# A transformer block with two recurrences: x times W_ih for up to four steps at once, kept in an SBUF ring

## The reference, cut to what matters

```
def cell(h, x):                                   # GRU, one time step
    i_r, i_z, i_n = split(x @ W_ih + b_ih, 3)     # x: 64 x 512, W_ih: 512 x 1536
    h_r, h_z, h_n = split(h @ W_hh + b_hh, 3)
    r, z = sigmoid(i_r + h_r), sigmoid(i_z + h_z)
    n = tanh(i_n + r * h_n)
    return (1 - z) * n + z * h

def derivative(q, p, drive):                      # oscillators
    dq = q - q**3 / 3 - p + drive + tanh(q) @ coupling.T + bias
    dp = EPSILON * (q + ALPHA - BETA * p)
# four derivatives (Runge-Kutta) and a clip for each time step;
# drive of step t is x + (the GRU's h of step t)
```

## Time and profile before

| | |
|---|---|
| median of three runs | 1514.97 us (1504.56 to 1516.10) |
| the profiled execution | 1517.27 us, its span 1515.2 us |
| granted TensorE clock, mean | 0.988 |
| TensorE busy | 1453.9 us, 96% |
| VectorE busy | 1275.0 us, 84% |
| ACT busy | 902.3 us, 60% |
| GpSimd busy | 768.6 us, 51% |

### The profile page before, as it was taken

One profiled execution on the slowest core, in us unless ns is written; L12 is line 12 of the kernel. 1 busy time (PEld: TensorE's weight loads), 2 busy tenths in 40 slices (PEclk: granted clock), 3 DMA queues, 4 the chain that ended last, 5 costly groups with the idle time before them and its releaser, 6 DMA issues.

```text
span 1515.2 us, 94439 instructions
## 1 busy us (share of the span) xinstructions
PE 1453.9 (96%) x41966; PEld 1279.7 (84%) x41966; DVE 1275.0 (84%) x3095; ACT 902.3 (60%) x2753; POOL 768.6 (51%) x916
## 2 busy tenths in 40 slices
PE   4799999999999999999999999999999999999997
PEld 2366766666766669999999999999999999999996
DVE  6888888778888776788888889889888888888887
ACT  5567766757767743555555555555555555555553
POOL 2567777757677756443444344344444434434432
PEclk8899999999999999999999999999999999999999
DMA  7477777767777772000000000000000000000000
GB/s 258 82 158 167 162 154 161 166 146 169 170 171 176 153 163 79 12 11 15 15 12 15 15 12 15 15 12 15 16 15 11 15 15 12 15 15 12 15 15 14
DMA packets 188216, 108.74 MB, mean 72 GB/s; under 512 B 134272, under 2 KB 165184, under 8 KB 187808
## 3 DMA queue, kind: packets, MB, share of 16 engines
q1 hardware_dynamic: 187360, 102.45, 28.7%
q10 hardware_dynamic: 448, 0.25, 0.1%
HBM read 50.65 MB, written 11.67 MB: 41 GB/s over the span
## 4 chain that ended last, share of the span: by engine, by line
PE 79%; DVE 9%; DMA 4%; issue 3%; SPq 2%; ACT 1%; POOL 1%; DVEq 0%; ACTq 0%; POOLq 0%
PE psB L1463 35%; PE psA L1492 15%; PE psQ L1174 10%; PE psA L1497 8%; PE psQ L1220 4%; PE psO L1266 3%; DMA first<-qn 2%; DMA PT<-front 2%; PE psO L1254 2%; PE psB L1202 1%; DVE psA L830 1%; SPq L325 1%; DVE qn L770 1%; DVE room L801 1%; DVE oT L893 1%
## 5 line engine op out<-in xcount | busy, mean ns | idle before, releaser
L1463 PE MATMUL psB<-first,Wx 128*128 128x64 f16 x9216 | 290.7, 193 | 1.8 <-issue 1.3
L1492 PE MATMUL psA<-ts,Cp 128*128 128x64 f16 x8160 | 281.0, 193 | 7.1 <-ACT ts L1563 6.4
L1463 PE MATMUL psB<-first,Whh 128*128 128x64 f16 x9072 | 286.2, 193 | 0.8 <-POOL first L1928 0.5
L1174 PE MATMUL psQ<-Wx,front 128*128 128x512 f16 x1152 | 280.1, 391 | 5.5 <-DVE front L982 4.6
L1463 PEld LDWEIGHTS psB<-first,Wx 128*128 128x128 f16 x9216 | 278.0, 98 | 2.8 <-issue 2.4
L1463 PEld LDWEIGHTS psB<-first,Whh 128*128 128x128 f16 x9072 | 273.7, 98 | 1.4 <-POOL first L1928 0.6
L1492 PEld LDWEIGHTS psA<-ts,Cp 128*128 128x128 f16 x8160 | 256.3, 98 | 8.3 <-ACT ts L1563 7.2
L1563 ACT ACTIVATE ts<-qst 128x256 f16<-128x256 f32 x192 | 80.1, 417 | 298.0 <-DVE qst L1676 298.0
L1174 PEld LDWEIGHTS psQ<-Wx,front 128*128 128x128 f16 x1152 | 107.5, 100 | 124.3 <-issue 12.3
L1928 POOL TENSOR_TENSOR en<-rz,dn 128x256 f32<-128x256 f32 x64 | 46.7, 730 | 259.5 <-issue 256.8
L1497 PE MATMUL psA<-ts,Cp 128*128 128x64 f16 x4080 | 161.2, 193 | 0.0
(11 more groups left out here) (199 smaller groups left out, 2899.8 us busy)
## 6 DMA issues: line engine op xcount, KB each, us to landing
rows<-rows_dram SPq DMA_DIRECT2D x64, 256.0 KB, 4.3
front<-in_x SPq DMA_DIRECT2D x32, 256.0 KB, 4.3
XR<-in_x_turned SPq DMA_DIRECT2D x32, 256.0 KB, 4.8
out<-ob SPq DMA_DIRECT2D x63, 128.0 KB, 1.8
x<-x SPq DMA_DIRECT2D x29, 224.0 KB
Whh<-in_W_qkv SPq DMA_DIRECT2D x12, 256.0 KB, 8.3
room<-in_W_hh SPq DMA_DIRECT2D x12, 256.0 KB, 2.7
room<-in_W_ih SPq DMA_DIRECT2D x12, 256.0 KB, 2.9
```

The lines of the kernel that those rows point to most:

```text
L1174: last = mm(psQ[:, n, :], xn[p.u][:, i, c, :], Wqkv[:, j, c, n * D:(n + 1) * D], start=(c == 0 and t == 0), stop=(c == KC - 1 and t == 2))
L1463: last = mm(o, W_[:, i, c, g * PART:(g + 1) * PART], src[:, j, c, :], start=False, stop=False, skip_group_check=True)
L1492: mm(psF[:, s % 2, m, :], Cp[:, i, c, m * PART:(m + 1) * PART], ts_[:, 0, c, :], start=(c == 0 and m == 0 and i == 0), stop=False, skip_gr ...
```

## The change

x times W_ih leaves the gates' PSUM. The cells 3 to 62 are put in groups (`CELLS`): [3], [4, 5], [6, 7], twelve groups of four from 8 to 55, [56, 57], [58, 59], [60], [61], [62]. The products of a group are made together, with up to 4 x 64 = 256 columns, into one of two banks of psQ (`products_of_group`), in the steps of `STEPS_OF`: group 0 in step 0, group 1 in step 1, group 2 in steps 2 and 3, group 3 (cells 8 to 11) in steps 4 and 5, the groups of cells 12 to 55 in four steps each (6 to 49), [56, 57] in steps 50 to 53, [58, 59] in 54 and 55, [60] in 56 and 57, [61] in 58, [62] in 59, none in 60. A group has 12 chunks of 12 products; a step does 12 divided by the number of its group's steps, the first half of them between stages 0 and 1, the rest between stages 1 and 2. ACT copies each chunk with its bias to the SBUF ring gx (`keep`), the first half of a step's chunks behind tanh_n and the others behind seed_n. A chunk waits until the chunk two before it has been copied. Cells 0 to 2 and 63 stay as they were. `seed_rz` copies from gx, `seed_n` seeds h's half alone, gate_b adds from gx. seed_n now stands behind high_h and the square of stage 2. The square sq and PA move to SBUF, nn to the half of psN that x's part held. In the front three pairs of semaphores are merged into two, with the same waits.

```diff
+    LEN = 4
+    CELLS = [[3], [4, 5], [6, 7]] + [list(range(n, n + LEN)) for n in range(8, 56, LEN)] + [[56, 57], [58, 59], [60], [61], [62]]
+    xg = [sb(f"xg{u}", [PART, 2, KC, LEN, B], F16) for u in range(2)]
+    gx = [sb(f"gx{u}", [PART, GC, LEN, B]) for u in range(2)]
+    GROUP = {n: g for g, cells in enumerate(CELLS) for n in cells}
+    STEPS_OF = [[0]] + [list(range(CELLS[g - 1][0] - 2, CELLS[g][0] - 2)) for g in range(1, len(CELLS))]
+    assert sorted(GROUP) == list(range(3, T - 1)) and sum(STEPS_OF, []) == list(range(T - 4))
+
+    def chunks_in(n):
+        for g, steps in enumerate(STEPS_OF):
+            if n in steps:
+                per = GC // len(steps)
+                return g, range(steps.index(n) * per, (steps.index(n) + 1) * per)
+        return None, range(0)
+
+    def turned_in(n):
+        for g, steps in enumerate(STEPS_OF):
+            if n in steps:
+                cells = CELLS[g + 1] if g + 1 < len(CELLS) else [T - 1]
+                return [c for k, c in enumerate(cells) if steps[k * len(steps) // len(cells)] == n]
+        return []
+
+    def place_of(n):
+        g = GROUP[n] if n < T - 1 else len(CELLS)
+        return g, (n - CELLS[g][0] if n < T - 1 else 0)
+
+    def xs_of(n):
+        if n < 3:
+            return xs1 if n == 1 else xs
+        g, k = place_of(n)
+        return xg[g % 2][:, :, :, k, :]
...
-    psRZ, psN, psF, psT, psQ, psH, psE = (bank(*k) for k in (("psB", 0), ("psB", 1), ("psA", 0), ("psA", 1), ("psQ", 0), ("psQ", 1), ("psQ", 2)))
+    psRZ, psN, psF, psT, psE = (bank(*k) for k in (("psB", 0), ("psB", 1), ("psA", 0), ("psA", 1), ("psQ", 2)))
+    psX = banks["psQ"]
     psS = banks["psO"][:, :, :].rearrange("p c n -> p (c n)").rearrange("p (v c b) -> p v c b", v=2, c=KC)
-    th, sq = psT[:, 0, :, :], psQ[:, 0, :, :]
-    nn, PA = psH[:, 0, :, :], psH[:, 1, :, :]
+    th, sq = psT[:, 0, :, :], sb("sqs", F)[:, :, :]
+    nn, PA = psN[:, 1, :, :], sb("PA", F)[:, :, :]
...
+        def products_of_group(g, parts):
+            N = len(CELLS[g]) * B if parts else 0
+            for m, c in parts:
+                j = g * GC + m
+                if c == 0:
+                    if m == 0:
+                        pe.wait_ge(S["xs_ready"], CELLS[g][-1] + 1)
+                    need(pe, S["gx_kept"], j - 1)
+                for k, (i, jj) in enumerate(TERMS):
+                    last = mm(psX[:, j % 2, 0:N], Wih[:, i, c, m * PART:(m + 1) * PART],
+                              xg[g % 2][:, jj, c, :, :].rearrange("p t b -> p (t b)")[:, 0:N],
+                              start=(c == 0 and k == 0), stop=(c == KC - 1 and k == 2), skip_group_check=True)
+                if c == KC - 1:
+                    last.then_inc(S["gx_done"], 1)
...
         def step(t):
+            g, ms = chunks_in(t.n)
+            parts = [(m, c) for m in ms for c in range(KC)]
             if t.n:
                 stage(t, 0)
-            gi_front(t.n + 2)
+            if t.n == 0:
+                gi_front(2)
+            products_of_group(g, parts[:len(parts) // 2])
             stage(t, 1)
-            gi_back(t.n + 2)
+            if t.n == 0:
+                gi_back(2)
+            products_of_group(g, parts[len(parts) // 2:])
             stage(t, 2)
+            pe.wait_ge(S["seeded_rz"], t.n + 3)
+            pe.wait_ge(S["seeded_n"], t.n + 3)
             gh_front(t.n + 2)
...
-                act.wait_ge(S["gi_done"], n)
-            a((xs1 if n == 1 else xs)[:, 0, :, :].rearrange("p c b -> p (c b)"), xr(n)).then_inc(S["xs_hi"], 1)
+                need(act, S["gx_done"], (place_of(n)[0] - 1) * GC)
+            a(xs_of(n)[:, 0, :, :], XR[:, :, :, n]).then_inc(S["xs_hi"], 1)
 
         def seed_rz(n):
             need(act, S["sig_done"], n)
-            a(both(psRZ), both(seedRZ)).then_inc(S["seeded_rz"], 1)
+            if n in GROUP:
+                g, k = place_of(n)
+                act.wait_ge(S["gx_kept"], (g + 1) * GC)
+                a(psRZ.rearrange("p v c b -> p (v c) b"), gx[g % 2][:, 0:2 * KC, k, :]).then_inc(S["seeded_rz"], 1)
+            else:
+                a(both(psRZ), both(seedRZ)).then_inc(S["seeded_rz"], 1)
 
         def seed_n(n):
-            need(act, S["bn_done"], n)
-            a(both(psN), both(seedN)).then_inc(S["seeded_n"], 1)
+            need(act, S["h_done"], n)
+            if n in GROUP:
+                a(flat(psN[:, 0, :, :]), flat(seedN[:, 0, :, :])).then_inc(S["seeded_n"], 1)
+            else:
+                a(both(psN), both(seedN)).then_inc(S["seeded_n"], 1)
+
+        def keep(g, ms):
+            N = len(CELLS[g]) * B if ms else 0
+            for m in ms:
+                j = g * GC + m
+                act.wait_ge(S["gx_done"], j + 1)
+                if m == 0 and g > 1:
+                    act.wait_ge(S["bn_done"], CELLS[g - 2][-1] + 1)
+                    act.wait_ge(S["seeded_rz"], CELLS[g - 2][-1] + 1)
+                bias = seedRZ[:, m // KC, m % KC, 0:1] if m < 2 * KC else seedN[:, 1, m - 2 * KC, 0:1]
+                a(gx[g % 2][:, m, :, :].rearrange("p t b -> p (t b)")[:, 0:N], psX[:, j % 2, 0:N], ACT.Identity, bias=bias).then_inc(S["gx_kept"], 1)
...
             tanh_n(0)
+            high_h(0)
             seed_n(1)
-            high_h(0)
             high_xs(2)
+            high_xs(3)
             of_p(0)
...
+            keep(g, ms[:half])
             tanhs(t, 2)
             if has(t, 2):
                 high_h(t.n + 1)
             square(t, 2)
-            if has(t, 3):
-                high_xs(t.n + 3)
+            if has(t, 2):
+                seed_n(t.n + 2)
+            keep(g, ms[half:])
+            for n in turned_in(t.n):
+                high_xs(n)
...
-            v.tensor_tensor(an[:, :, :], psN[:, 0, :, :], rz[:, 0, :, :], ALU.mult).then_inc(S["an_done"], 1)
+            to = psN[:, 0, :, :] if n in GROUP else an[:, :, :]
+            v.tensor_tensor(to, psN[:, 0, :, :], rz[:, 0, :, :], ALU.mult).then_inc(S["an_done"], 1)
 
         def gate_b(n):
             dve.wait_ge(S["an_done"], n + 1)
             need(dve, S["nn_done"], n)
-            v.tensor_tensor(bn[:, :, :], psN[:, 1, :, :], an[:, :, :], ALU.add).then_inc(S["bn_done"], 1)
+            if n in GROUP:
+                g, k = place_of(n)
+                dve.wait_ge(S["gx_kept"], (g + 1) * GC)
+                v.tensor_tensor(bn[:, :, :], psN[:, 0, :, :], gx[g % 2][:, 2 * KC:GC, k, :], ALU.add).then_inc(S["bn_done"], 1)
+            else:
+                v.tensor_tensor(bn[:, :, :], psN[:, 1, :, :], an[:, :, :], ALU.add).then_inc(S["bn_done"], 1)
...
             low_xs(2)
+            low_xs(3)
```

More of the change, by code:

```diff
@@ L550, in high_qk_turned @@
         def high_qk_turned(p, n):
-            act.wait_ge(qk_T, 1)
+            act.wait_ge(end_turned, 1)
             need(act, sc_done, p.n)
@@ L612, in high_p @@
         def high_p(p, h):
-            act.wait_ge(p_T, p.n - N2.n)
+            act.wait_ge(end_turned, 1 + p.n - N2.n)
             need(act, mix_done, p.n)
@@ L779, in low_qk_turned @@
             else:
-                v.tensor_tensor(qkT[:, 1, 1, :, :], t, qkT[:, 1, 0, :, :], ALU.subtract).then_inc(qk_ready, 1)
+                v.tensor_tensor(qkT[:, 1, 1, :, :], t, qkT[:, 1, 0, :, :], ALU.subtract).then_inc(end_ready, 1)
         def scale_x(p):
@@ L845, in low_p @@
             if h == 1:
-                lo.then_inc(pt_ready, 1)
+                lo.then_inc(end_ready, 1)
         def least(p):
@@ L854, in subtract_least @@
             if p.n == N0.n:
-                dve.wait_ge(p_T, 1)
+                dve.wait_ge(end_turned, 2)
             else:
@@ L1152, in turn_qk @@
                     last = nc.tensor.transpose(psA[:, n, c * PART:(c + 1) * PART], sq[:, n, c * PART:(c + 1) * PART], ident[:, :])
-            last.then_inc(qk_T, 1)
+            last.then_inc(end_turned, 1)
         def project(p, n, chunks=range(KC)):
@@ L1180, in turn_p @@
             pe.wait_ge(p_done, p.n * 2 + 2)
-            pe.wait_ge(qk_ready, 1)
+            pe.wait_ge(end_ready, 1)
             if p.n == N0.n:
-                pe.wait_ge(pt_ready, 1)
+                pe.wait_ge(end_ready, 2)
             for j in range(HEADS // 2):
@@ L1186, in turn_p @@
                                            S[:, 2 * j:2 * j + 2, :].rearrange("p h k -> p (h k)"), ident[:, :])
-            last.then_inc(p_T, 1)
+            last.then_inc(end_turned, 1)
         def scores(p):
             if p.n == NP - 1:
-                pe.wait_ge(qk_ready, 1)
+                pe.wait_ge(end_ready, 1)
             else:
@@ L1531, in last_steps @@
             pe.wait_ge(S["seeded_rz"], cell + 1)
-            gate_products(Wih, xs, 1, range(0, KC + 1))
+            gate_products(Wih, xs_of(cell), 1, range(0, KC + 1))
             stage(t, 1)
-            gate_products(Wih, xs, 1, range(KC + 1, 2 * KC))
+            gate_products(Wih, xs_of(cell), 1, range(KC + 1, 2 * KC))
             pe.wait_ge(S["seeded_n"], cell + 1)
```

(19 more changed lines are left out.)

8 lines of the change are left out of this document (4 added, 4 removed).

## The result

**3.1% slower: 1558.54 us (median of 4 runs, 1555.03 to 1564.97) against 1512.93 (1504.56 to 1516.1), a ratio of 1.0307, 95% interval 1.0267 to 1.0347.** The forecast was 1565, made against 1515.0. The profiled execution took 1560.97 us, its span 1559.2, 44.0 more than before's 1515.2.

The account below looks back on a forecast made before the run. TensorE was taken to bound the kernel, 14.00 of 14.065 us a full step, with 0.29 us of slack in the VectorE chain. Terms summed to +49.6 on the profiled 1517.3, 1566.9, less 2.3 for the median: 1565; range 1535 to 1578.

Parts of the forecast that it names:

- the slack: Full step before stage 3: TensorE never waits, and the VectorE and tanh chain is ready 0.29 us before it is needed.
- Part 1: Products of x in full steps: 256 columns cost 109.1 ns each, saving 0.13 us in F1 and F2, 0.27 a step.
- Part 2: Square and PA in SBUF: cubic 2 waits for GpSimd's low half of h, +0.43 us; full step 14.16, 0.10 more.
- rival A: Full steps: no contention between cubic 2 and GpSimd, steps of 13.78 us, so 1546 us; chance 0.20.
- Rival B: GpSimd wins twice: cubic 0 waits too, q2 0.3 us late in 57 steps, so 1582 us; chance 0.08.
- Part 3: ACT in full steps: three more copies (0.51 us at 256 columns), a smaller seed and the same turning all hide.
- Part 4: Steps not full: chunks wait for ACT's late copies; start, steps 0 to 5 and 54 to 59 +43.5 us together.
- the last cell: Step 61: it waits for its seed, now behind tanh 2, h and the square, partly absorbed at stage 3; +1.2 us.
- the waits before third chunks: Half steps of three or more chunks: the third waits for ACT's first copy; 1.1 and 1.4 us in step 1.
- Rival C: TensorE's own sum sets the time everywhere, 60 cells costing 237.7 us instead of 252, so about 1505 us; chance 0.10.

Follow-up runs that it names:

- experiment 2: The kernel before with only the square and PA moved to SBUF; 1520.86 us, 1.0028 of the kernel before.
- Kernel 5: The changed kernel with GpSimd's product for h's low half moved ahead of the sums for the next cell's input; 1544.29 us, 1.0215 of the kernel before.
- the first of 6: The change with chunks side by side in a bank, TensorE not before seeds at the ends, h's low half first, groups of four cells; 1517.61 us, 1.0020.
- experiment 1: Two kernels: the change with cubic 2 one VectorE instruction later (1546.34 us, 1.0214), and placed further back (1548.33 us, single run).
- experiment 3: The changed kernel with several chunks of a half step side by side in one bank, copied after the visit; 1532.43 us, 1.0120 of the kernel before.
- 4: On top of experiment 3, step 0's own products go before those waiting for the seed, the last cell's n products after stage 2; 1529.86 us, single run.
- experiment 6: Two kernels: the change with the edits of experiment 3, 4 and Kernel 5 together, in groups of four cells (1517.61 us) and of two (1508.64 us, 0.9965).

## Why the prediction was right, and where its terms were off

**What bounds the kernel, and the slack.** Right. The slack was the 0.29 us between tanh and stage 3, and experiment 2 shows it: there 0.35 us of delay cost 0.07. Kernel 5 and the first of 6 show the step without the meeting: stage 3 at S0+10.24 (prediction: 10.24 without contention, step 13.74; measured 13.75), where tanh and TensorE's own products arrive together. No full step of any kernel went below 13.73. The prediction said 13.71, but its own product times (9.80 us of 64 columns and 3.93 of 256) make 13.73.

**Part 1, 256 columns.** 109.2 ns for 109.1, stages 1 and 2 at S0+3.37 and 6.73 for a loss of 0.13 each: as computed from 64, 128 and 512 columns in other code.

**Part 2, the meeting of cubic 2 and the low half.** The mechanism was right, rival A (no contention) fell with the 0.73 us of cubic 2, and experiments 1, 2 and 5 show it from three sides. The size was off by 0.08 us a step: q4 came 0.35 later and not 0.43, cubic 2 took 0.73 us and not some 0.84. I let the cubic end 0.35 us after the low half; the trace has 0.29, and the low half itself ended 0.02 sooner than I had it (X was held back by 0.12 and not 0.18). The Trainium skill ("SBUF — State Buffer", Who interferes with whom) calls the port pair that the two engines share an exclusive lock, and says that issue order decides who blocks. The trace agrees for the cubic behind X (1.06 us) and behind the low half (0.73): it comes second and ends after the other. But not all of its 0.42 us waits. In experiment 1 the cubic began 0.13 us before the low half's end and lost nothing, and 0.42 less 0.13 is the 0.29 seen in the other two meetings. This term made the forecast 3.0 us too long over steps 6 to 49 (2.7 in the table, since the kernel before took 0.3 less there than 44 times 14.06) and 0.5 in the steps 50 to 53 and 60. The other 0.7 there is the pause in step 52 of the kernel before, not a term of mine. Rival B (GpSimd also wins at cubic 0) fell too: cubic 0 took 0.62 us, but q2 stayed at S0+1.7 (1089.90).

**Part 3, ACT's copies in full steps.** They hid: experiment 3 removed all waiting for them and left full steps at 14.06. A 256-column copy took 0.46 us for my 0.51.

**Part 4, steps that are not full.** Nearly the whole loss: the start, steps 0 to 5 and 54 to 59 were forecast at +43.5 us together and measured +43.1. Single steps were within 0.25 us but for step 58. That the waits before third chunks are the cause was only argued there; experiment 3 shows it, 22.8 us of the stretch. The size of step 58 (19.65 for 18.35) and of the last cell (+2.8 for +1.2) I had wrong, for one cause in part: after 1.9 us of waiting TensorE came back at half its clock. This is the change in step 58, the wait and what follows it:

```profile
1464.66:1467.30 2.64, 1.56 (x48) 1.44 (x49) 2.64 (x8) 1.93 (x8) 0.20 (x1) 1.00 0.01 3
1467.30:1469.90 2.60, 2.60 (x56) 2.60 (x53) 0.01 (x1) 0.51 (x2) 0.52 (x1) 0.51 0.00 0
1469.90:1472.50 2.60, 1.24 (x28) 1.11 (x25) 2.32 (x7) 1.86 (x7) 1.49 (x2) 0.84 0.03 6
```

In experiment 5, where the same wait of 1.88 us was not followed by a drop, step 58 took 18.45, 0.1 over the forecast's 18.35. In step 61, experiment 1's two kernels had the same wait of 1.93 us without a drop and took 14.70, 1.2 more than before's 13.50: again the forecast's term.

**Rival C.** TensorE's own sum, 1505 us, was within reach only by removing what the rival named. With the copies' waits gone and the meeting gone the change stands at 1517.6. Some 12 us remain. More than half of them are the lead that light steps can't give back, as part 4 said of steps 50 to 53: with the lead cut to two cells, steps 4 and 5 alone give 7.7. Another 2.7 were the meeting of X and cubic 2. What makes up the rest no run separates. (The rival's own sum of the 60 cells, 237.7 us, adds up to 237.4; nothing hangs on it.)

## What to carry to other kernels

A helper engine's place in its own order, not its instruction's length, sets when it frees a buffer: a copy of 0.36 us cost about 1 us of waiting, twice in each step of six chunks, because it stood behind a tanh whose input came late. Give TensorE as much room as half a step of its products needs, or make the copy's turn come first. Work that is done ahead is paid for at once and given back only where the engine is again the bound; if another chain holds the light steps, keep the lead as short as the batching gain allows. And when an operand moves from PSUM to SBUF, look for every instruction of GpSimd that runs at the time, in each kind of step, since moving one clears one meeting and can make another.

## What the runs showed of the hardware that I had not expected

TensorE's clock fell from the 2.4 to the 1.2 GHz level after waits of 1.9 to 2.4 us that followed steady work, but not each time, and in one kernel where it didn't in another. Step 61's wait of 1.93 to 1.97 us was followed by a drop in the change (clock 0.55) and in kernels 3 and 5, and by none in the two of experiment 1. Step 58's wait of 1.88 to 1.90 us was followed by one in the change and in both of experiment 1, by none in kernel 5. Step 60's wait of 2.07 us for tanh was followed by a drop in kernels 1 (both), 3, 4 and 5, which took 14.80 to 15.14 us there, and by none in the change (14.03) and in the two of experiment 6. All kernels wait 2.4 us ahead of stage 0 of step 63; in the kernel before and in both of experiment 6 the clock fell right behind it, in both of experiment 1 some 1.1 us into the stage, in the others not at all. The first window below is the kernel before's behind that wait, the second the change's:

```profile
1500.00:1502.00 2.00, 2.00 (x42) 2.00 (x40) 1.00 (x4) 0.00 (x0) 1.41 (x2) 0.50 0.01 4
```

```profile
1544.00:1546.00 2.00, 2.00 (x70) 2.00 (x71) 1.65 (x5) 0.83 (x3) 0.85 (x2) 1.00 0.00 0
```

42 products in 2 us against 70: that is the 0.8 us by which the change's step 63 was shorter. A drop cost 0.8 to 1.6 us where it fell, and 0.4 in step 63 of experiment 1. So the executions compared differ by such drops, and by pauses at full clock such as the 0.65 us in step 52 of the kernel before; a term of a microsecond in one step of one profile may be nothing else. What decides whether it drops is open; no run varied the wait alone.
